# Second-order attention: one state product over two runs of columns, and fewer waits on TensorE

## The reference

```python
q, k, v = (x @ Wq, x @ Wk, x @ Wv)          # 16 heads of 32 columns each
def step(carry, qkv):                        # one token
    C_prev = GAMMA * C_QV
    k_C = einsum('bhk,bhkv->bhv', k_t, C_prev)
    G = GAMMA * G + k_t[..., :, None] * k_C[..., None, :]
    S_K = GAMMA * S_K + k_t[..., :, None] * k_t[..., None, :]
    C_QV = C_prev + q_t[..., :, None] * v_t[..., None, :]
    o_t = einsum('bhk,bhkv->bhv', q_t, einsum('bhij,bhjv->bhiv', S_K, C_QV) - G)
return outs @ Wo
```

## Time and profile before

| | us |
|---|---|
| median of 3 runs (3536.5 to 3544.11) | 3537.71 |
| the profiled execution, device time | 3529.74 |
| its span, first to last instruction | 3527.8 |
| second-order attention in the trace, about | 1505 to 2720 |

### The profile page before, as it was taken

How to read it: one execution, slowest core, us unless ns; L and a number is a source line. 1 busy time by engine, 2 the same in 40 slices (tenths; PEclk the granted TensorE clock), 3 DMA queues, 4 the chain that set the end, 5 groups by cost and what they waited for, 6 DMA issues and landing times. The chain is left out here.

```text
span 3527.8 us, 137586 instructions
## 1 busy us (share of the span) xinstructions
PE 3262.7 (92%) x55606; PEld 2885.2 (82%) x55606; DVE 2266.3 (64%) x6633; ACT 2043.5 (58%) x6370; POOL 1375.0 (39%) x2094
## 2 busy tenths in 40 slices
PE   8938999789965999989999999999998999999998
PEld 7938999777745999978888888888887888888877
DVE  6574555678866555546655555545555788888887
ACT  5555565555535565444444444434443699999996
POOL 5755565300004665423333333333333633333325
PEclk9979999999986999999999999999999999999999
DMA  4144343611134443420000000000001133333333
GB/s 131 49 146 104 89 96 66 169 32 49 56 107 159 95 93 84 105 60 4 4 4 4 4 4 4 4 4 3 4 4 35 31 120 118 118 107 102 104 99 101
DMA packets 202923, 235.34 MB, mean 67 GB/s; under 512 B 17968, under 2 KB 182976, under 8 KB 202304
## 3 DMA queue, kind: packets, MB, share of 16 engines
q1 hardware_dynamic: 177728, 192.99, 17.4%
q0 software_dynamic: 24576, 33.57, 5.6%
HBM read 147.46 MB, written 79.04 MB: 64 GB/s over the span
## 5 line engine op out<-in xcount | busy, mean ns | idle before, releaser
L2518 ACT ACTIVATE wa_S<-wa_S,wa_top 128x192 f32<-128x192 f32 x1024 | 462.7, 475 | 36.6 <-DVE wa_top L2614 36.6
L2057 POOL TENSOR_TENSOR so_OT<-so_O,so_OT 128x128 fp32r<-128x128 f32 x256 | 117.5, 459 | 745.5 <-ACT so_OT L1889 745.5
L1974 DVE TENSOR_TENSOR so_raw<-so_rows,so_masks 128x1024 f32<-128x1024 f32 x256 | 313.4, 1224 | 105.8 <-PE so_rows L1662 98.6
L1968 DVE COPY so_O<-so_bankX 128x128 f32<-128x128 f32 x256 | 74.6, 291 | 416.9 <-PE so_bankX L1775 347.3
L2614 DVE CUSTOM_DVE_ANT_0 wa_S<-wa_bank,wa_band 128x192 f32<-128x192 f32 x1024 | 294.9, 348 | 3.5 <-issue 3.4
L1897 ACT ACTIVATE so_KW<-so_bankU 128x128 f32<-128x128 f32 x256 | 71.2, 278 | 321.1 <-PE so_bankU L1669 321.1
L650 POOL DMA_INDIRECT sum_dram<-y,rows x128 | 223.6, 1747 | 29.4 <-issue 27.2
L2406 PE MATMUL wa_bank<-ident,wa_S 128*128 128x128 f32 x1536 | 221.2, 277 | 7.7 <-ACT wa_probT L2525 4.7
L2518 ACT ACTIVATION_READ_ACCUMULATOR wa_S<-wa_S,wa_top 128x1 f32 x1024 | 222.5, 217 | 0.0
L1691 PE MATMUL so_bankJ<-so_xnT,so_w 128*128 128x256 f32 x1500 | 210.2, 290 | 7.5 <-DVE so_xnT L1948 7.2
L728 ACT ACTIVATE m2e_hT<-m_bank,m2e_bias 128x256 fp32r<-128x256 f32 x256 | 126.9, 496 | 150.2 <-PE m_bank L680 144.2
(11 more groups left out here) (459 smaller groups left out, 9730.9 us busy)
## 6 DMA issues: line engine op xcount, KB each, us to landing
m_w_raw<-in_L_ffn_W_dram SPq DMA_DIRECT2D x64, 512.0 KB, 3.8
wa_V<-wa_V_dram SPq DMA_DIRECT2D x256, 128.0 KB, 3.0
sum_dram<-X SPq DMA_DIRECT2D x16, 1024.0 KB, 4.7
X<-sum_dram SPq DMA_DIRECT2D x16, 1024.0 KB, 8.3
wa_V_dram<-wa_V_new SPq DMA_DIRECT2D x32, 512.0 KB, 3.8
wa_V_rest<-wa_V_dram SPq DMA_DIRECT2D x128, 128.0 KB, 3.3
X<-in_L_attn_a_x_dram SPq DMA_DIRECT2D x8, 1024.0 KB, 11.7
xn_dram<-m2r_xn SPq DMA_DIRECT2D x16, 512.0 KB, 4.5
```

What stands on the lines that cost most here:

```text
L1968: nc.vector.tensor_copy(O[:, t % UT], bX[:, O_AT]).then_inc(s_["O_copied"], 1)
L1974: nc.vector.tensor_tensor(AB[:, t % 2].rearrange("p h m t -> p h (m t)"), rows4[:, :, 0:2 * P], masks[:].rearrange("p m t -> p (m t)")[:, ...
L2057: nc.gpsimd.tensor_tensor(OT[:, 1, t % (2 * UT)], O[:, t % UT], OT[:, 0, t % (2 * UT)].bitcast(F32), ALU.subtract).then_inc(s_["O_ready"], 1)
L2518: nc.scalar.activation(S[:, n % 2, z], S[:, n % 2, z], ACT.Exp, bias=top[:, n % 2, z:z + 1], scale=-1.0, accum_out=sums[:, i % 2, SET * c ...
```

## The change

K and W of a unit move into one buffer of 320 columns: K in columns 0 to 127, minus W in 128 to 255, 64 columns unused. W's columns of head h stand at `(h + 1) % 4`, so head h's K and W are two runs of 32 columns that lie 160 apart for h = 0 to 2, and one run of 64 for h = 3. `state_products` multiplies the decayed keys with both at once: four matmuls of 64 columns in place of eight of 32. The rest leaves waits out on TensorE: those that were waited for earlier in its own order, and those that stand behind another wait on an engine that works in order.

```diff
-        KW, KQe = sb("KW", [P, 2, 2, P]), sb("KQe", [P, 2, 2, P])
+        KW_all, KQe = sb("KW", [P, 2, 2 * P + 2 * DK]), sb("KQe", [P, 2, 2, P])
+        KW = KW_all[:, :, 0:2 * P].rearrange("p b (m t) -> p b m t", m=2)
+        KW_pairs = KW_all[:].rearrange("p b (m x) -> p b m x", m=2)
                 def keys_queries(t):
                     at = place(t)
-                    pe.wait_ge(s_["QT_ready"], halves_to(tile(t)))
-                    pe.wait_ge(s_["KT_ready"], halves_to(tile(t)))
-                    if t >= 1:
-                        pe.wait_ge(s_["AB_ready"], t)
-                    if t >= 2:
-                        pe.wait_ge(s_["PT_ready"], t - 1)
+                    if t % (2 * UT) == 0:
+                        pe.wait_ge(s_["KT_ready"], halves_to(tile(t)))
                 def turn_W(t):
                     pe.wait_ge(s_["WT_ready"], t + 1)
-                    pe.wait_ge(s_["U_ready"], t + 1)
                 def turn_KQ(t):
                     at = place(t)
-                    if t >= 1:
-                        pe.wait_ge(s_["U_ready"], t)
+                def keys_and_W(t, h):
+                    if turned_rows(h).start == 0:
+                        return KW_all[:, t % 2, h * DK:(h + 2) * DK]
+                    return KW_pairs[:, t % 2, :, head_rows(h)]
                 def state_products(t):
-                    for m, of in ((0, head_rows), (1, turned_rows)):
-                        for h in range(HG):
-                            nc.tensor.matmul(bX[head_rows(h), HID + m * DK:HID + (m + 1) * DK], KQe[:, t % 2, 0, head_rows(h)],
-                                             KW[:, t % 2, m, of(h)], start=True, stop=True, tile_position=(0, h * DK))
+                    for h in range(HG):
+                        nc.tensor.matmul(bX[head_rows(h), HID:HID + 2 * DK], KQe[:, t % 2, 0, head_rows(h)],
+                                         keys_and_W(t, h), start=True, stop=True, tile_position=(0, h * DK))
-                    if 1 <= t <= NU:
+                    if t < NU:
+                        pe.wait_ge(s_["KQe_ready"], t + 1)
+                    elif t == NU:
                         pe.wait_ge(s_["W_ready"], t)
-                    if t < NU:
-                        pe.wait_ge(s_["K_ready"], t + 1)
-                        pe.wait_ge(s_["KQe_ready"], t + 1)
                     if 2 <= t <= NU:
-                        pe.wait_ge(s_["O_copied"], t - 1)
-                        pe.wait_ge(s_["S_ready"], updates_to(t - 2))
-                        if mixes_in_states_to(t) >= 1:
+                        if updates(t - 2):
+                            pe.wait_ge(s_["S_ready"], updates_to(t - 2))
+                        else:
+                            pe.wait_ge(s_["O_copied"], t - 1)
+                        if mixes_in_states_to(t) > mixes_in_states_to(t - 1):
                             pe.wait_ge(s_["x_ready"], 2 * mixes_in_states_to(t))
-                    if t < NU and carries(t):
+                    if t < NU and carries(t) and t % UT == 0:
                         pe.wait_ge(s_["QTg_ready"], carrying_tiles_to(tile(t)))
                         pe.wait_ge(s_["KTg_ready"], carrying_tiles_to(tile(t)))
```

## The result

The changed kernel takes 3511.4 us (median of 4 runs, 3508.27 to 3512.2); the kernel before, run beside it, 3537.33 us (3536.5 to 3544.11). The ratio is 0.9921, 95% interval 0.9904 to 0.9938: 26 us less, where 13.3 were forecast. The profiled execution took 3508.27 us, 21.5 less than that of before.

What follows compares the result with a forecast made beforehand. TensorE's instruction stream was taken to bound the kernel. Savings of 2.0 + 5.3 + 0 + 6.0 = 13.3 us off 3537.7 gave 3524.4, predicted as 3524.5 us, range 3513 to 3541.

Steps and rivals of the forecast that it cites:

- part 4: TensorE's instruction supply: waits for issue mostly vanish as held events go and packet borders move on; 6.0 of 7.1 us saved.
- Part 1: State products: eight records of 64 columns replace sixteen of 32, 0.009 us less in 224 units, 2.0 us.
- rival (C): State products slower, two runs of columns read at half rate: 22 us, 3546; chance 0.14 shared with the slower-supply rival.
- Part 2: Wait behind VectorE's residual add in turn 2: fewer events after it, 0.22 us less in 24 units, 5.3 us.
- Part 3: Other removed waits, turns of kind 3 to 6: seven events become one, nothing saved on TensorE's stream itself.
- Rival (D): TensorE's loads were held back by their waits, not by the tile-shape change: time near 3478; chance 0.03.
- (A): Instruction-supply waits stay; only joined state products and the residual-add wait gain: 3530.4; chance 0.20.
- (B): Slower instruction supply: borders moving by 17 cause 50 waits, 33 us for 7.1, 3556; chance 0.14 with the half-rate rival.
- (E): TensorE gives the time back at another wait: no change, 3538; chance 0.10.
- three signs of being wrong: L1739 still waits 0.4 us or more, 64-column sets take over 0.07 us, or waits for issue exceed 7 us.

Runs made afterwards that it cites:

- refilled: The kernel before with the state products joined and W's four matmuls issued once more, 261 instructions in a steady unit, held waits kept: 3558.52 us, ratio 1.0058.
- no hold with x last: The kernel before with W's and K's waits replaced by long-ended ones, KQe's on the weight load, the residual add's written last: 3511.53 us, ratio 0.9924.
- x on the load: The changed kernel with the wait for the residual add written first in turn 2, so the weight load carries it: 3503.96 us, ratio 0.9907.
- no hold: The kernel before with W's and K's waits replaced by two that ended long ago, KQe's first on the weight load: 3523.32 us, ratio 0.9940.
- products only: The kernel before with only the state products joined, 245 instructions a unit for 261, every wait kept: 3514.81 us, ratio 0.9928.
- after, held: The changed kernel with KQe's wait written behind that for the states, so an event is held for it again: 3510.76 us, ratio 0.9902.
- borders at 40: The kernel before with head 3's state products joined in six of eight units and 28 more warm-up matmuls: 3550.21 us, ratio 1.0034.
- many borders: The kernel before with head 3's state products joined in six of eight units and 32 more warm-up matmuls: 3517.52 us, ratio 0.9935.

## Why the prediction was right in direction and wrong in size

The measured time lies below the forecast range. The failing step is the size of part 4, "I take 6.0 of the 7.1 us".

- **Part 1 (2.0 us) held.** Usual units are 0.004 to 0.017 us shorter with the products joined, about 0.013 x 224 = 3 us. The priced narrow set holds as well: refilled's two sets cost 0.065 us a unit, 0.032 each for a forecast 0.031. Two runs of columns cost nothing seen, so rival (C) is out. (Its 3546 counts part 1's 2.0 us as saved as well; its own figures give 3548.)
- **Part 2 (5.3 us) held.** Turn 2 went from 5.61 to 5.38 us, 24 x 0.23 = 5.5, of which 0.4 is part 1's. The step of 0.11 us per event shows at four orders: 1.10, 0.88, 0.77 and 0.67 us from the x transpose to the first product (before, after, no hold with x last, x on the load).
- **Part 3 (0) held.** With the waits alone removed, turns 3 to 7 stay at 4.60 to 4.61 us. Rival (D) is out.
- **Part 4 was sized wrong, twice.** First, the idle column isn't the loss: the execution with 7.1 us of waits for issue was late by 12.4. The earlier trace rows had it: 953 matmuls in 42 us for 1116 elsewhere, 15% fewer or 6.1 us in that stretch alone, of which busy time shows 4.7. Second, that execution was a mild draw: one of two rows of late units was on. Time less late units is 3517.3, 3520.2 and 3517.4 us in three profiles of before, so the median of 3537.3 holds some 17 to 20 us of them. After has 0.6. I took the 8 us between profile and median as an offset that the change leaves alone; it was the same loss.
- **Part 4's mechanism held in its main part.** "A border crossed shortly before such a hold" and "borders move by 17 per unit and linger nowhere" are borne out: without the hold no rows (no hold), with the hold and quick borders none (products only; after, held), with the hold and borders that linger at 33 to 49 a row of 24 (borders at 40). I had the place too wide at first, as "many borders" showed. The prediction's "asked for only when the hold ends" is what the packets of borders at 40 show, some 1.2 us behind the hold's end; why most packets at such places are asked for in time, and a row's aren't, stays open.
- **Rivals (A), (B) and (E) are out.** (B) asked for 50 waits from borders moving by 17; after, held, has two late units.

The sum with these sizes: 5.1 + 3 + 17 to 19 = 25 to 27 us, for 26 measured. None of the three signs of being wrong came true (L1734 waits 7.1 / 24 = 0.30 us, a joined set takes 0.06, no wait for issue is left): they watched the idle column too, and that column didn't hold the miss.

The Trainium skill's section cited above says that a crossing is mostly hidden. That holds for most of the 245 borders of before; in its third profile 37 late units cost 34.0 us.

## What to carry to other kernels

Size a stall by work done per time (matmul counts in equal stretches, unit to unit), not by the idle column, and take a second profile where runs spread by more than the change is worth. An order of waits is free to change: put the wait that ends last on the instruction itself, so that no event stands behind it or is held. Where the instructions of a loop's unit come near 256 and an event is held in it, the count and even the warm-up's length decide whether packet borders linger in a bad place.

## What the runs showed of the hardware

Four warm-up matmuls less ahead of the stage, with nothing else changed, cost 33 us in the median: 3550.21 for 3517.52, on two chips (1.0034 and 0.9935 of before's time there). Once a packet was late, the next ones were too for as long as the borders stayed: 24 borders in a row, 22 units of 0.6 to 1.6 us, at a granted clock of 1.00. Their packets started some 1.2 us after the end of a held event, where packets on time started 0.05 to 1.34 us after the border.
